# Eight z tiles and six silu's among the last turned y, a signal for each turned end, the last state update by halves, and the first feed-forward evictions ahead of the taps

## What is computed

```
h = layernorm(x); xn = rmsnorm(h)
z, K, V = projections of xn
u = silu(causal convolution of V, 4 taps)
alpha, omega, dt, beta, gates = small projections of u      (32 heads)
scan over the tokens, per head a state S of 16 x 2:
    Sr = rotation(A11, A12) S
    S  = Sr + beta * (v - sum(k * Sr)) * k
y = sum(Q * S);  y = groupnorm(y) * silu(z) + D * u
x = x + layernorm(h + y @ out_W.T)
pool over tokens -> router -> two of eight experts, weights by softmax
x = x + layernorm(sum over the two experts of gelu(x2 @ W1 + b1) @ W2 + b2), x2 = layernorm(x)
```

## Time and profile before

| what | value |
|---|---|
| median of three runs | 1441.14 us (1440.51 to 1441.62) |
| the profiled execution's own time | 1439.7 us |
| its span, first to last instruction | 1437.8 us |
| TensorE busy | 1251.7 us, 87% |
| VectorE busy | 1126.5 us, 78% |
| ScalarE busy | 799.3 us, 56% |
| GpSimd busy | 174.0 us, 12% |
| mean granted TensorE clock | 0.955 |

### The profile page before, as it was taken

How to read it: one execution, slowest core, us unless ns; L and a number is a source line. 1 busy time by engine, 2 the same in 40 slices (tenths; PEclk the granted TensorE clock), 3 DMA queues, 4 the chain that set the end, 5 groups by cost and what they waited for, 6 DMA issues and landing times. The chain is left out here.

```text
span 1437.8 us, 14657 instructions
## 1 busy us (share of the span) xinstructions
PE 1251.7 (87%) x4248; PEld 739.7 (51%) x4248; DVE 1126.5 (78%) x1824; ACT 799.3 (56%) x2747; POOL 174.0 (12%) x77
## 2 busy tenths in 40 slices
PE   5987788863999789798899999899997798999997
PEld 3543333332555456465565565555554464666664
DVE  5989899988999968789899999779999684511011
ACT  4896666613788855957422223346888555333332
POOL 0000155500122200000011111001222000000000
PEclk9999899986999899899999999999999999999999
DMA  6004111010311021601232231313110105232221
GB/s 234 1 8 176 59 59 48 26 59 1 118 45 59 30 108 46 254 23 44 70 106 78 84 103 59 103 59 118 44 59 30 59 1 197 92 132 73 74 73 73
DMA packets 54400, 110.88 MB, mean 77 GB/s; under 512 B 4785, under 2 KB 40114, under 8 KB 52274
## 3 DMA queue, kind: packets, MB, share of 16 engines
q1 hardware_dynamic: 54322, 109.97, 21.5%
HBM read 81.64 MB, written 28.31 MB: 76 GB/s over the span
## 5 line engine op out<-in xcount | busy, mean ns | idle before, releaser
L772 PE MATMUL ps<-kz 128*128 128x256 f32 x1024 | 246.4, 384 | 15.4 <-ACT kz L1148 10.7
L772 PEld LDWEIGHTS ps<-kz 128*128 128x128 f32 x1024 | 195.9, 192 | 100.4 <-issue 62.0
L758 PE MATMUL ps<-kz 128*128 128x512 f32 x512 | 242.7, 597 | 0.3 <-DVE small L1963 0.3
L1148 ACT ACTIVATE kz<-ps,small 128x512 f32<-128x512 f32 x128 | 87.3, 685 | 276.9 <-PE ps L758 276.7
L648 PE MATMUL ps<-wshare,uT 128*128 128x512 f32 x512 | 230.1, 603 | 5.4 <-DVE work L1767 5.3
L648 PEld LDWEIGHTS ps<-wshare,uT 128*128 128x128 f32 x512 | 96.5, 193 | 119.0 <-issue 110.4
L997 ACT ACTIVATE work<-ps,coef 128x16 f32<-128x16 f32 x768 | 129.3, 389 | 40.4 <-DVE work L1757 26.9
L566 PE MATMUL ps<-wshare,xnT 128*128 128x512 f32 x256 | 121.7, 620 | 34.0 <-ACT ps L854 33.8
L1214 POOL TENSOR_TENSOR work<-work 128x1024 f32<-128x1024 f32 x28 | 66.9, 2390 | 594.1 <-DVE work L1675 363.3
L758 PEld LDWEIGHTS ps<-kz 128*128 128x128 f32 x512 | 98.0, 192 | 77.4 <-issue 71.4
L1975 DVE TENSOR_TENSOR kz<-ps,b_s 128x256 f32<-128x256 f32 x16 | 6.3, 414 | 135.9 <-PE ps L772 135.9
(11 more groups left out here) (289 smaller groups left out, 2118.4 us busy)
## 6 DMA issues: line engine op xcount, KB each, us to landing
kz<-in_w SPq DMA_DIRECT2D x128, 256.0 KB, 3.0
kap_d<-kz SPq DMA_DIRECT2D x26, 512.0 KB, 2.7
kz<-kap_d SPq DMA_DIRECT2D x26, 512.0 KB, 3.2
kz<-in_x SPq DMA_DIRECT2D x3, 2048.0 KB, 8.2
v_d<-kz SPq DMA_DIRECT2D x4, 1024.0 KB, 4.5
wshare<-in_wq SPq DMA_DIRECT2D x2, 2048.0 KB, 8.1
coef<-in_x SPq DMA_DIRECT2D x2, 2048.0 KB, 7.8
work<-v_d SPq DMA_DIRECT2D x3, 1024.0 KB, 6.9
```

What stands on the lines that cost most here:

```text
L758: t = mm(ps[:, 4 + i % 2, :], w1_r[r][:, k, (f % 2) * P:(f % 2 + 1) * P], x2T[:, k, n * 512:(n + 1) * 512], start=(k == 0), stop=(k == KM ...
L772: t = mm(ps[:, 6 + q // 2, (q % 2) * DM:(q % 2 + 1) * DM], hbuf(i)[:, q * P:(q + 1) * P], w2_r[r][:, f % 2, :], start=(f == 0 and q % 2 == ...
L1148: af(hbuf(i), ps[:, 4 + i % 2, :], ACT.Gelu, bias=b1_s[:, f // FT, f % FT:f % FT + 1]).then_inc(h_done, 1)
```

## The change

- **z tiles and silu's.** PE makes z tiles 0 and 1 ahead of the turned y 13, 2 and 3 ahead of y 14, 4 to 6 ahead of y 15 and 7 behind it (before: 0 and 1 behind y 13, 2 behind y 14, 3 behind y 15). ACT makes silu 0 and 1 ahead of the eviction of y 13, 2 and 3 behind it, 4 and 5 behind y 14, 6 ahead of y 15, and 7 behind the fourth normed y. The first four silu's go to `wshare`, where the query weights lay. Behind the group norm PE makes z tiles 8 to 10 and 11 to 12 ahead of the first and second four output tiles, then 13 to 15.
- **Turned ends.** `end_turned` and `mt_ready` count each tile.
- **Last state update.** PE signals its first half (`half_ready`); DVE multiplies the halves one after the other.
- **First value.** In batch 0 too DVE makes it; ACT's `first_value(b, 0)` is gone.
- **Feed-forward.** ACT evicts units 0 and 1 ahead of the second block of taps and units 2 and 3 behind it; the wait for the last eviction stands in `turn_starts`.

```diff
         def szb(i):
-            if i == 2:
-                return work[:, 5120:5632]
+            if i < KI:
+                o = (2560, 3072, 3584, 0)[i]
+                return wshare[:, o:o + 512]
             o = (2048, 2560, 0, 512)[i % 4]
...
                     for c in range(2):
                         t = mm(ps[:, 4 + 2 * a + c, :], ident[:] if i == 0 else nident[:], X[:, a, c],
                                start=(i == 0), stop=True, skip_group_check=True)
+                    if i == L - 2 and a == 0:
+                        t.then_inc(half_ready, 1)
...
                     pe.wait_ge(end_ready, b * 2 + o + 1)
-                    if o:
-                        pe.wait_ge(mt_ready, b * 2 + 1)
                     for c in range(3):
+                        if o and c > 0:
+                            pe.wait_ge(mt_ready, b * 6 + c)
                         for g in range(KI):
...
-                    t.then_inc(end_turned, 1)
+                        t.then_inc(end_turned, 1)
 
             def turn_starts(b):
                 pe.wait_ge(scan_done, b + 1)
+                if b > 0:
+                    pe.wait_ge(f_used, b * NCH)
...
-                    for i in range(*((4, 10), (10, 14), (14, NV), (NV, NV))[n]):
+                    for i in range(*((8, 11), (11, 13), (13, NV), (NV, NV))[n]):
...
                     experts(b - 1, UNITS[L] + 1, NF)
-                    pe.wait_ge(f_used, b * NCH)
                 queries(b)
...
                 for o in range(2):
-                    act.wait_ge(end_turned, b * 2 + o + 1)
                     for i in range(3):
+                        act.wait_ge(end_turned, b * 6 + 3 * o + i + 1)
                         t = af(mts[:, o, i].rearrange("p s q -> p q s"),
                                ps[:, end_bank(b, 3 * o + i), :].rearrange("p (q s) -> p q s", s=NS), ACT.Copy)
-                    t.then_inc(mt_ready, 1)
+                        t.then_inc(mt_ready, 1)
...
                     act.wait_ge(cv_ready, b + 1)
-                    first_value(b, 0)
                     key_bias(b, 1)
...
-                if b > 0:
-                    dve.wait_ge(cv_ready, b + 1)
-                    value(0)
+                dve.wait_ge(cv_ready, b + 1)
+                value(0)
...
+                    if b == 0 and not more:
+                        dve.wait_ge(half_ready, 1)
+                        at["h"] = mark(tt(X[:, 0], M[:, 0], k, MUL))
+                        dve.wait_ge(state_ready, i)
+                        tt(X[:, 1], M[:, 1], k, MUL).then_inc(x_ready, 1)
+                        after(at["h"])
```

More of the change, by code:

```diff
@@ L239, in build @@
         cv_ready = sem("cv_ready")
+        half_ready = sem("half_ready")
         z0_ready = sem("z0_ready")
@@ L554, in token_u @@
                 if i == L:
-                    pe.wait_ge(mt_ready, b * 2 + 2)
+                    pe.wait_ge(mt_ready, b * 6 + 6)
                     pe.wait_ge(state_used, 1)
@@ L668, in queries @@
                         turn_y(b, j - 3)
-                turn_y(b, L - 3)
                 gate_tile(b, 0)
                 gate_tile(b, 1)
+                turn_y(b, L - 3)
+                gate_tile(b, 2)
+                gate_tile(b, 3)
                 turn_y(b, L - 2)
-                gate_tile(b, 2)
+                for i in range(4, 7):
+                    gate_tile(b, i)
                 turn_y(b, L - 1)
-                gate_tile(b, 3)
+                gate_tile(b, 7)
             def gate_tile(b, i):
@@ L928, in silu_u @@
                         af(ug, ug, ACT.Silu).then_inc(u_ready, 1)
+                experts(b - 1, 0, 2)
                 taps(b, 1)
-                experts(b - 1, 0, 2)
+                experts(b - 1, 2, UF)
+                silu_u(0)
                 taps(b, 2)
-                silu_u(0)
-                experts(b - 1, 2, UF)
+                silu_u(1)
                 taps(b, 3)
-                silu_u(1)
                 silu_u(2)
@@ L1031, in passes @@
                         second_value(b, j + 2)
+                    if j == L - 3:
+                        silu(b, 0)
+                        silu(b, 1)
+                    if j == L - 1:
+                        silu(b, 6)
                     act.wait_ge(yt_ready, b * L + j + 1)
@@ L1040, in passes @@
                     t.then_inc(yt_done, 1)
[L1041 to L1044, removed]
+                    if j in (L - 3, L - 2):
+                        silu(b, 2 if j == L - 3 else 4)
+                        silu(b, 3 if j == L - 3 else 5)
                     if j == 6:
@@ L1054, in silu @@
                 act.wait_ge(z_ready, b * NV + i + 1)
-                if i == 0:
+                if i == 4:
                     act.wait_ge(turned_ready, b * L + L)
-                if i == 3:
+                if i == 6:
                     act.wait_ge(yp_ready, b * L + L)
-                if i >= 4:
+                if i >= 8:
                     act.wait_ge(y2_ready, b * NV + i - 3)
@@ L1091, in x2_normed @@
                            ).then_inc(x2a_ready, 1)
-                yn(0)
-                yn(1)
-                yn(2)
-                for i in (3, 4, 5, 6, 7):
-                    silu(b, i)
+                for i in range(8):
+                    if i == 4:
+                        silu(b, 7)
                     yn(i)
@@ L1669, in pass_1 @@
                         M = ps[:, 4:8, :].rearrange("p (a c) n -> p a c n", a=2)
-                        dve.wait_ge(state_ready, i)
                     else:
@@ L1674, in pass_1 @@
                     dve.wait_ge(k_ready, b * L + i + 1)
-                    tt(X, M, kb, MUL).then_inc(x_ready, 1)
+                    if b == 0 and not more:
[4 more added lines that the diff above has]
+                        after(at["h"])
+                    elif b == 0:
+                        dve.wait_ge(state_ready, i)
+                        tt(X, M, kb, MUL).then_inc(x_ready, 1)
+                    else:
+                        tt(X, M, kb, MUL).then_inc(x_ready, 1)
                     if b == 0 and i == 1:
@@ L1730, in chunk_scan @@
                     turn(b, 1)
-                dve.wait_ge(mt_ready, b * 2 + 2)
+                dve.wait_ge(mt_ready, b * 6 + 6)
                 done = n_chain[0]
```

## The result

The changed kernel takes **1417.1 us** (median of four runs, 1416.8 to 1417.7) beside 1440.8 us for the kernel before: a ratio of 0.9836, with an interval of 0.9819 to 0.9853. That is 23.7 us less; the forecast was 27.2 us less in the profiled execution. The span of the profiled one went from 1437.8 to 1415.1 us, 22.7 us less, so 4.5 us of the sum are missing, and as will be seen they are not missing evenly.

A forecast was written before the change was run, and what follows sets the result against it. No engine bounds the whole span; gains lie at joints between stages. Terms 2 x 7.8 + 3.2 + 3.6 + 1.05 + 2.1 + 1.65 = 27.2 us off 1439.7 give 1412.5, median 1.4 above: 1413.9; range 1410 to 1418, wider 1409 to 1423.5.

The forecast's parts named there:

- Part 1, (a): End of pass 2, each batch: a shorter PE gap keeps the clock full at y 15, 1.6 us less.
- part 1: End of pass 2, each batch: eight z tiles and six silu's among the last turned y's, 7.8 us less per batch.
- clock rival: PE's new gaps of about 3 us lower its clock, y 15 and output tiles run half speed: 1421.3 us, chance 0.17.
- Part 1, (b): Behind the group norm: fewer z tiles left, output tiles start earlier and stay ahead of DVE, 6.3 us less per batch.
- signs of being wrong: PE's clock row at 0.5 in the tail, DVE waiting for the residual's load, or a pass 1 or 2 growing.
- The floor of part 1: DVE's gating needs the residual, loaded behind the last product; it lands at 1131.9 against a need at about 1132.0.
- Parts 2 and 3: Turned ends signalled singly, last eviction's wait moved behind batch 1's first query: 3.2 us in batch 0, 3.6 in batch 1.
- Parts 4 and 5: Batch 0: last state update by halves, 1.05 us less, and first value on DVE, 2.1 us less.
- Part 6: Start of batch 1: first feed-forward evictions ahead of the taps bring the head projections earlier, 1.65 us less.
- the absorbed one: Gains at batch 1's start, in the halves and first value vanish in later scan waits: 1418.7 us, chance 0.08.
- the change doesn't do what it says: Tail: silu 4 to 6 wait, PE keeps tiles 7 to 10; 5 us won per batch: 1419.5 us, chance 0.08.
- The slower one: Clock falls in a new gap and stays down from y 15 to output tile 7: 1465.7 us, chance 0.03.

The follow-up runs named there:

- z11_in_gap: The changed kernel with z tile 11 moved ahead of the first four output tiles and tiles 12, 13 ahead of the second four; 1410.6 us, ratio 0.9796.
- tail_alone: The kernel before with only the eight z tiles and six silu's moved among the last turned y's; 1429.0 us, ratio 0.9918.
- ends_alone: The kernel before with only a signal for each turned end and the last feed-forward eviction's wait moved behind the first query; 1430.3 us, ratio 0.9939.

## Why the prediction was right, and where it was not

The forecast of 1413.9 us was 3.2 us too low, inside its own range, and the direction and the size hold. By its steps:

- **Part 1, (a)**: right in size. y 15 takes 2.05 and 1.95 us; the lead grows by 1.7 and 1.4 us, forecast 1.6. Not all of it is the part's own: four batches of kernels without part 1 have the same 2.05 us, each behind a slow y 14. In all traces y 15 took 3.1 to 3.8 us after each gap of 4.6 us, and 2.05 or less after 3.1 us or less. But the gap alone doesn't decide it. y 14 was slow (2.7 to 3.7 us) in 13 of the 15 batches in which its gap was 2.4 to 3.0 us, and fast in all 13 with 2.2 us or less. In the changed kernel y 13 or y 14, or both, are slow in every batch, after the new gaps of 2.5 to 2.8 us that the clock rival named; VectorE waits for neither, which is the luck in this step. The row that the rival rests on, "after a gap of this kind", stood behind a gap of 7.45 us, not of 3.
- **Part 1, (b)**: the start of the output tiles is right (4.6 us closer in batch 0, 4.4 in batch 1, forecast 4.6). The step that failed is the next: "From there PE's output tiles are ahead of DVE." They were counted with the 7.07 us of the old trace, in which PE came to them without a break, while the change itself puts an idle time of 3.2 us there. They took 8.86 and 10.03 us, and the term of 6.3 us less was worth 4.5 and 3.4. The clock rival named this mechanism and place, with 2.1 us per batch; z tile 11 in the gap shows 1.6 and 2.7 us. What was wrong was to leave it a rival: the prediction itself put the gap at about 3 us, and no row had full speed behind a gap that long, the rows having full speed behind 2.21 us and half behind 4.62. Of the prediction's own signs of being wrong one came, the 0.50 in the clock row of the tail.
- **The floor of part 1**, the residual's load, held: in batch 0 VectorE's first gate waits 1.06 us with the load named as last, in batch 1 0.95 us for ACT, so by these two rows it costs some 0.1 us.
- **Parts 2 and 3**: right. 3.1 and 2.5 + 1.4 us, forecast 3.2 and 3.6. The copies take 5.4 us, as summed.
- **Parts 4 and 5**: right in this trace. 1.0 and 2.3 us (0.8 and 2.2 alone), forecast 1.05 and 2.1; the second trace of the changed kernel has 2.9 and 1.2 in the same stretches.
- **Part 6**: the order of the work on ACT came as summed (PE starts 1.4 us closer to the router), but the term had the projections at the speed of the earlier trace rows. PE's new gap is 2.75 us, their first records run at half clock, and 0.7 of 1.65 us is left. A filled gap gives 1.9 us more at this place. The table load was 1.28 us with work right behind it, as in its row. The 2.66 us of the Trainium skill (ScalarE: Activation LUTs, What ACT_TABLE_LOAD costs) are the same 1.28 us and a drain, and no such drain shows here.
- **The rivals**: the absorbed one is refuted in the traces of the changed kernel: of its three terms two came whole, and part 6 fell short at its own place, by a slow clock and not by a later wait. That the change doesn't do what it says is refuted by the output tiles' start, 4.6 and 4.4 us closer, and by z11_in_gap, where the tail gives 7.8 and 7.6 us per batch, the forecast's number. The slower one needed the clock to stay down through 13.6 us of extra time per batch; it was back within the first four output tiles in every trace that had it low there.

So the missing 4.5 us are 4.4 in the two tails and 0.95 in part 6, by the clock behind a gap that the change made, and 1.5 in the router; 1.7 at the second key tile and 0.7 of small ones came back. The router's and the key's entries hang on which execution of the kernel before is taken. That the total came so near, 22.7 for 27.2 us, owes nothing to them, as they nearly cancel.

## What to carry to other kernels

When a change lets an engine run ahead, read off the sum where TensorE will now stand idle, and carry both prices for what follows a gap of 2.4 to 3.3 us: in these traces such gaps had half clock behind them in most cases, and never full clock at the first output tiles. Then ask whether another engine waits for the work behind the gap. Work that stands behind it anyway, moved into the gap, wins twice. Here one z tile did what three useless products did, and turned 23.7 us into about 30. A difference of 1 or 2 us between two traces in a place that the change does not touch should be sought in a second trace of the same kernel before it is explained.

## What the runs showed of the hardware

- The clock of TensorE behind an idle time is not a fixed price. After 2.06 us the key tile took 5.40 us in one execution and 3.70 in another of the same kernel; after 3.2 us the output tiles were slow in both traces of the changed kernel and in `tail_alone`, in each batch. A slow piece can take the next one's place: behind a slow y 14 (3.59 to 3.68 us) y 15 took 2.05 us in four batches, after idle times of 3.00 to 3.09 us.
- Products that nobody reads hold the clock as well as work does (8 records of the update in 3.70 instead of 5.83 us, the output tiles in 7.17 us, with work 7.07), and cost nothing where they end before the next work is ready: 0.6 us ahead of the output tiles, which started at the same moment.
- The executions of one kernel split by this. Those of `ends_alone` took 1428.7 to 1429.0 us at a mean granted clock of 0.959, and 1434.6 and 1434.9 at 0.952 (a sixth 1431.5 at 0.956): 6 us, nearly as much as the parts under test. Gains measured alone on such a kernel don't add up to the gain of all.
